# Some filler matmuls moved onto the two 64-row halves of the array, between the score matmuls; a new table of steps; three filler banks in PSUM

## The reference

```
x_proj = silu(xn @ W1 + b1); u, v, q, k = split(x_proj, 4)      # 16 heads of 16
scores = einsum('bqhd,bkhd->bhqk', q, k)
attn   = silu(scores) / S                                        # no softmax
y      = layernorm(einsum('bhqk,bkhd->bqhd', attn, v) * u) @ W2 + b2
h      = gelu(layernorm(xn) @ ternary(w1).T + b1)                # 256 -> 1024
out    = layernorm(h) @ ternary(w2).T + b2                       # 1024 -> 256
x + y + out
```

## Time and profile before

| | |
|---|---|
| median of 3 runs | 1492.84 us |
| the profiled execution | 1493.36 us, span 1491.6 us |
| granted TensorE clock, mean | 0.997 |
| TensorE (PE) busy | 1464.8 us, 98% |
| ScalarE (ACT) busy | 1208.9 us, 81% |
| VectorE (DVE) busy | 895.3 us, 60% |
| chain that ended last | PE 88%, DVE 5%, ACT 4% |

### The profile page before, as it was taken

One profiled execution on the slowest core, in us unless ns is written; L12 is line 12 of the kernel. 1 busy time (PEld: TensorE's weight loads), 2 busy tenths in 40 slices (PEclk: granted clock), 3 DMA queues, 4 the chain that ended last, 5 costly groups with the idle time before them and its releaser, 6 DMA issues.

```text
span 1491.6 us, 25963 instructions
## 1 busy us (share of the span) xinstructions
PE 1464.8 (98%) x9942; PEld 784.7 (53%) x9942; DVE 895.3 (60%) x1719; ACT 1208.9 (81%) x1273; POOL 97.4 (7%) x197
## 2 busy tenths in 40 slices
...
GB/s 248 81 128 57 15 132 65 130 57 15 156 71 100 58 15 156 95 104 29 30 155 99 113 1 59 126 129 84 1 89 110 142 57 5 115 81 142 29 1 29
DMA packets 67996, 123.49 MB, mean 83 GB/s; under 512 B 12832, under 2 KB 14496, under 8 KB 66976
## 3 DMA queue, kind: packets, MB, share of 16 engines
...
q10 hardware_dynamic: 160, 0.26, 0.1%
...
## 4 chain that ended last, share of the span: by engine, by line
PE 88%; DVE 5%; ACT 4%; issue 1%; DVEq 1%; DMA 0%; ACTq 0%
PE outs L1101 30%; PE scores L1079 22%; PE fill L1136 10%; PE fill L1170 9%; PE fill L1154 7%; PE fill L1186 3%; PE fill L1163 3%; ACT attn L636 3%; PE fill L1145 2%; DVE tmp L917 1%; PE fill L1126 1%; DVE hid L900 1%; ACT hid L681 1%; DVE st L813 1%; ACT L636 1%
## 5 line engine op out<-in xcount | busy, mean ns | idle before, releaser
L636 ACT ACTIVATE attn<-scores 128x1024 f32<-128x1024 f32 x1024 | 991.4, 1023 | 225.3 <-PE scores L1079 220.6
L1101 PE MATMUL outs<-attn,V 128*32 128x512 f32 x4096 | 494.3, 600 | 0.0
L1079 PE MATMUL scores<-QS,KS 64*128 64x512 f32 x2048 | 387.7, 452 | 8.3 <-ACT attn L636 7.0
L1079 PEld LDWEIGHTS scores<-QS,KS 64*128 64x128 f32 x2048 | 163.0, 184 | 300.4 <-ACT attn L636 241.5
L1101 PEld LDWEIGHTS outs<-attn,V 128*32 128x32 f32 x4096 | 107.2, 109 | 235.8 <-issue 235.1
L900 DVE SCALAR_TENSOR_TENSOR hid<-fill,ratq,fb1b 128x512 f32<-128x512 f32 x128 | 96.1, 751 | 77.6 <-PE fill L1154 72.3
L917 DVE TENSOR_TENSOR tmp<-fill,l2g 128x512 f32<-128x512 f32 x128 | 88.6, 692 | 88.6 <-PE fill L1163 81.1
L1170 PE MATMUL fill<-Wq,hgh 128*128 128x256 f32 x504 | 128.2, 292 | 2.0 <-DVE hgl L924 1.1
L1136 PE MATMUL fill<-xp,W1h 128*128 128x512 f32 x384 | 128.4, 416 | 0.5 <-DVE xp L949 0.5
L1170 PE MATMUL fill<-Wq,hgl 128*128 128x256 f32 x504 | 123.1, 282 | 0.0
L1170 PEld LDWEIGHTS fill<-Wq,hgh 128*128 128x128 f32 x504 | 95.8, 190 | 18.9 <-issue 14.6
(11 more groups left out here) (138 smaller groups left out, 1349.3 us busy)
## 6 DMA issues: line engine op xcount, KB each, us to landing
...
KS<-k_scratch SPq DMA_DIRECT2D x128, 128.0 KB, 3.2
KS<-k_scratch SPq DMA_DIRECT2D x256, 64.0 KB, 3.4
...
```

The lines of the kernel that those rows point to most:

```text
L636: nc.scalar.activation(attn_of(g)[:, 2 * hf:2 * hf + 2, :], SP[:, 2 * hf:2 * hf + 2, :], ACT.Silu).then_inc(s_silu, 1)
L1079: ins = mm(SP[:, j, :], KS[rows, pair, t * P:(t + 1) * P], QS[rows, pair - c * PPC, h * HALF:(h + 1) * HALF], start=True, stop=True)
L1101: ins = mm(OP[32 * j:32 * j + 32, g // RUN % 2, :], V[:, t, c * HPC // 2 + j, o * DH:o * DH + 2 * DH], attn_of(g)[:, n, :], start=(o == 0 ...
```

## The change

1. **Halves.** Where the pieces of a round are exactly one pair of a kind (`f1.t.0 f1.t.1`, `g.t.0 g.t.1`, `k q`, `u u`) or one `f2` alone, they are issued as matmuls with 64 contraction rows, two side by side, each into a bank of its own (`crossed`, `transposed`, `summed`). The first half of them stands ahead of the first pair of score matmuls of the next group, the second half between the first pair and the second. An `f2` in halves makes two partial sums in two banks, and VectorE adds both. An `f2` in halves waits for both of its `g` at its start; a whole one waited for the second in its middle.
2. **Where the next scores stand.** `scores(2n+2)` is issued at the end of round n instead of the start of round n+1, which is the same place in the stream. On ScalarE the steps of the halved pieces stand between the two SiLU instructions of that group.
3. **Banks.** `outs` has one bank instead of two, so the first `times_v` of each 16 groups waits for VectorE's `output`; `fill` has three banks instead of two. The setup matmuls of block 0 use the third.
4. **Table.** The order is new. In a middle block 11 of the 32 rounds are issued in halves: n = 2 (`k.1.0 q.1.0`), 6 (`u.1.0 u.0.0`), 9 (`k.1.1 q.1.1`), 10 (`f1.0.0 f1.0.1`), 24 and 30 (`k q` of the next block), and 19, 21, 23, 28, 31 (one `f2` each). Round 0 has four `zt` and both of the first `zs`; rounds 1, 3, 4, 5 one `a` each; rounds 7 and 8 one `u` each. Round 25 now has `g.5.0 g.5.1 v.0 gelu.3 v.1 xt.2 ln2.3`, round 26 `xn.3 nrm2.3 v.2 f2.5`; round 15 `f1.5.0 f1.5.1 f2.0 g.1.0 gelu.1 gelu.2 f1.6.0 g.1.1`, round 16 `ln2.1 f1.6.1 f2.1`. In block 0 the first five rounds have no filler piece. The last block has its `g` pairs in halves too.

```diff
-    "vs.1 a.2 zt.3",
+    "k.1.0 q.1.0 zs.2",
...
+def paired(pieces):
+    kinds = [s[0] for x, s in pieces]
+    if kinds == ["f2"]:
+        return SUM_IN_HALVES
+    if len(pieces) != 2 or pieces[0][0] != pieces[1][0]:
+        return False
+    (_, one), (_, two) = pieces
+    return kinds in (["f1", "f1"], ["g", "g"]) and one[1] == two[1] or kinds == ["k", "q"] and one[1:] == two[1:] or kinds == ["u", "u"]
...
-        OP = ctx.enter_context(nc.psum_tensor("outs", [P, 2, HALF], F32))
-        FP = ctx.enter_context(nc.psum_tensor("fill", [P, 2, HALF], F32))
+        OP = ctx.enter_context(nc.psum_tensor("outs", [P, HALF], F32))
+        FP = ctx.enter_context(nc.psum_tensor("fill", [P, FILLS, HALF], F32))
...
# ScalarE, body(b)
+                    nb, ng = next_group(b, 2 * n + 1)
+                    for hf in range(2):
+                        silu_half(b, 2 * n + 1, hf)
+                    steps = list(steps_of(b, n))
+                    group = pieces_of(b, n)[1]
+                    behind = steps.index(group[0]) if group else len(steps)
+                    for x, s in steps[:behind]:
                         step(x, *s)
+                    if nb < NB:
+                        silu_half(nb, ng, 0)
+                    for x, s in steps[behind:]:
+                        step(x, *s)
+                    if nb < NB:
+                        silu_half(nb, ng, 1)
...
# VectorE, step f2
+                    for k, turn in BANKS[x, me]:
+                        dve.drain()
+                        V_.scalar_tensor_tensor(out=part[:, t, :], in0=FP[:, k, 0:D], scalar=cq[:, 1:2],
+                                                in1=part[:, t, :], op0=ALU.mult, op1=ALU.add).then_inc(s_evac[k], 1)
...
# TensorE
-                if g % RUN == 0 and (b or g >= 2 * RUN):
+                if g % RUN == 0 and (b or g):
 
-                    pe.wait_ge(s_z, DC * NH * b + g // RUN - 1)
+                    pe.wait_ge(s_z, DC * NH * b + g // RUN)
...
+            def summed(steps, phase):
+                (x, step), = steps
+                t = step[1]
+                if phase == 0:
+                    wait_free(x, step)
+                pe.wait_ge(s_hg, 2 * T * x + 2 * t + 2)
+                for n in range(4):
+                    for w in (hgh, hgl):
+                        for half, (k, turn) in enumerate(BANKS[x, step]):
+                            rows = slice(half * P // 2, (half + 1) * P // 2)
+                            ins = mm(FP[:, k, 0:D], w[rows, phase, n * P:(n + 1) * P], Wq2[rows, 4 * phase + n, :],
+                                     start=phase == 0 and n == 0 and w is hgh, stop=phase == 1 and n == 3 and w is hgl)
+                            if phase == 1 and n == 3 and w is hgl:
+                                ins.then_inc(s_fill[k], 1)
...
             def body(b):
                 for n in range(ROUNDS):
-                    scores(b, 2 * n)
...
-                    scores(b, 2 * n + 1)
-                    for x, s in steps_of(b, n):
+                    for hf in range(2):
+                        scores(b, 2 * n + 1, hf)
+                    for x, s in full:
                         step(x, *s)
...
+                    for hf in range(2):
+                        if group:
+                            in_halves(group, hf)
+                        if nb < NB:
+                            scores(nb, ng, hf)
```

More of the change, by code:

```diff
@@ L138 @@
 LAST_ROUNDS = {
-    19: "ln2.2 f2.2",
+    19: "f2.2",
     20: "g.3.0 g.3.1 nrm2.2",
@@ L164 @@
 assert sorted(OPENING) == sorted(s for s in ORDER if is_next(s))
-EARLIER = {1: parsed("k.1.0")}
-MOVED = [s for n in sorted(EARLIER) for s in EARLIER[n]]
+SETUP_ROUNDS = 5
+DELAYED = [s for g in range(2 * SETUP_ROUNDS) for s in SLOTS[g] if s[0] in FILLERS and s[0] not in POST and not is_next(s)]
 def steps_of(b, n):
@@ L176, in steps_of @@
         return
-    if b == 0:
-        for s in EARLIER.get(n, ()):
-            yield b, s
+    if b == 0 and n == SETUP_ROUNDS:
+        for s in DELAYED:
+            yield 0, s
     for g in (2 * n, 2 * n + 1):
@@ L431, in last_piece @@
         def last_piece(bank):
-            return [xs for xs in PIECES if bank_of(*xs) == bank][-1]
+            return [xs for xs in PIECES if bank in [k for k, turn in BANKS[xs]]][-1]
         def last_a_tile(i, j):
@@ L730, in _ @@
                         sum_of_abs(i)
+            for hf in range(2):
+                silu_half(0, 0, hf)
+            act.wait_ge(s_const, 3)
+            step(0, "vs", 0)
             for b in range(NB):
@@ new lines, in transposed @@
+            def transposed(steps, phase):
+                if phase == 0:
+                    for x, step in steps:
+                        wait_free(x, step)
+                        wait_data(x, step)
+                for c in range(phase * HC // 2, (phase + 1) * HC // 2):
+                    for half in range(2):
+                        x, (kind, t, r) = steps[half]
+                        k = bank_of(x, (kind, t, r))
+                        toks = slice(half * P // 2, (half + 1) * P // 2)
+                        ins = nc.tensor.transpose(FP[:, k, c * P // 2:(c + 1) * P // 2], hid_of(t)[toks, c * P:(c + 1) * P],
+                                                  ident[toks, toks])
+                        if c == HC - 1:
+                            ins.then_inc(s_fill[k], 1)
@@ L1192, in setup_step @@
                 if g == 0:
+                    wait_evacuated(pe, *[xs for xs in PIECES[:len(OPENING)] if xs in OPENED and bank_of(*xs) == 2][-1])
                     pe.wait_ge(s_abs, 2)
                     pe.wait_ge(s_ones, 1)
-                    mm(OP[:, 1, 0:2], ones[:, :], asum[:, :], start=True, stop=True).then_inc(s_tot, 1)
+                    mm(FP[:, 2, 0:2], ones[:, :], asum[:, :], start=True, stop=True).then_inc(s_tot, 1)
                 elif g == 3:
```

315 lines of the change are left out of this document (197 added, 118 removed).

## The result

The changed kernel takes 1500.28 us (median of 6 runs, 1498.54 to 1504.59); the kernel before, beside it, 1492.94 us. The ratio is 1.0054 (95% interval 1.0042 to 1.0065): it is slower by half a per cent, where the prediction said 1479 and faster.

What follows compares the result with a forecast made beforehand. TensorE matmuls bound full rounds, a TensorE-ScalarE ring of 4.82 us the others. Six middle blocks at -2.3 us give -13.8, both end blocks -0.6: 1493.36 - 14.4 = 1479.0, said as 1479; 80% range 1464 to 1508.

Steps and rivals of the forecast that it cites:

- The floor of 4.82: Rounds with little filler take 4.82 us whatever is in them, as TensorE and ScalarE wait in a ring.
- the emptying stays: Rival: a score load's wait on ScalarE keeps it from loading ahead in halved rounds; +37 us, 1516; chance 0.05.
- the chain of ScalarE through the `gelu` rounds: ScalarE's steps make TensorE wait: rounds 15 and 16 take 16.9 us, rounds 25 and 26 take 16.1.
- ScalarE's price isn't due: Rival: rounds 15, 16, 25, 26 cost as before; -2 us per block more, 1463; chance 0.18.
- a slot of twice 0.118: Rival, dearer halves: 256-column half-height loads run in series; `f2` round 5.0 + 1.7 us, total 1547; chance 0.13.
- 5.28 - 0.42 = 4.86 ... so +0.14, 5.00: Halved `f2` round: saves 0.42 us of shape changes, loses 0.14 waiting for the first SiLU, takes 5.00.
- The `f1` pair likewise 5.0: Round 10, the `f1` pair in halves, takes 5.0 us like a halved `f2` round.
- 6.14 - 0.42 = 5.72: Rounds of `k q` or `u u` in halves fall from 6.14 to 5.72 us.
- So both together -0.6: Blocks 0 and 7: block 0 about -1.3 us; block 7 +1.9 in its last 13 rounds, -1.2 ahead; together -0.6.
- VectorE is late for the `f2` in halves: Rival: `f2` waits for both `g`; four per block, each 0.5 us late, +16 us, 1495; chance 0.14.
- a wait on `hgl`: Sign that would prove the forecast wrong: loads of half-height `f2` matmuls waiting on `hgl`; no size given.
- the way through DRAM that the prediction put at nothing: Next block's `k q` end a round later, with about two and a half rounds' cover before the keys' second half is due.

Runs made afterwards that it cites:

- e9: e11's order in rounds 0 to 22, the order of the kernel before from round 23 on and in the last block: 1474.51 us, ratio 0.9874.
- e5: The changed kernel with the last block's `g` pairs whole and an `f2` in halves waiting for its first `g` only: 1493.82 us, ratio 1.0011.
- e2: The changed kernel with the last block's `g` pairs whole instead of in halves: 1495.7 us, ratio 1.0024.
- e1: The changed kernel, new order and three banks kept, with every piece whole and none in halves: 1510.34 us, ratio 1.0122.
- e7: The changed kernel with every `f2` whole, other pieces in halves, and the last block's `g` pairs whole: 1502.48 us, ratio 1.0077.
- e11: The changed kernel in its new order, with the edits of e2, e3 and e5 together: 1484.25 us, ratio 0.9944.
- e3: The changed kernel with `f1.6.1` back in round 15 and `f2.5` in round 25 (last block: `f2.5` and `ln2.3` back too): 1485.89 us, ratio 0.9951.
- e4: The changed kernel's code with the order table of the kernel before, nothing else changed: 1485.36 us, ratio 0.9951.
- e6: The changed kernel with the order of the kernel before and the edits of e2 and e5: 1482.75 us, ratio 0.993.
- e8: The changed kernel with the order of the kernel before and no halves, leaving only the bank change and its code: 1489.08 us, ratio 0.9974.
- e10: e9 with the second pair's norm `nrm2.1` moved to round 16, ahead of `f2.1`'s sums on VectorE: 1478.69 us, ratio 0.9905.

## Why the prediction was wrong

By its own terms, for the fourth block:

| stretch | predicted | measured |
|---|---|---|
| rounds 0 to 10 | 56.5 | 57.38 |
| 11, 12 | 13.1 | 13.13 |
| 13, 14, 17, 18 | 19.3 | 19.27 |
| 15, 16 | 16.9 | 16.81 |
| 19 to 23 | 24.7 | 25.27 |
| 24 to 31 | 48.4 | 48.80 |

**Right.** The floor of 4.82 held in both kernels. A half-height pair of 256 columns costs 0.119, as one whole matmul; "the emptying stays" fell too. The third bank makes rounds 20 and 22 4.82. Above all the chain of ScalarE through the `gelu` rounds: what was taken out of rounds 15 and 25 came back as a wait in 16 and 26, at 16.81 and 16.00 for 16.9 and 16.1. The rival in which this price wasn't due fell in this order; e9 shows that another order avoids it.

**Slips of the sum.** The rival "ScalarE's price isn't due" starts from 32.3 us for rounds 15, 16, 25 and 26; the rows give 16.21 + 14.12 = 30.33. ScalarE's chain in round 15 adds up to 8.1, not 8.2. "0.4 x 11 x 8" is 35, and a slot of twice 0.118 makes an `f2` round 1.9 longer, not 1.7. None of them moves the forecast by more than 0.1 us a block.

**The failing step, in the middle blocks: the size of a halved round.** "5.28 - 0.42 = 4.86 ... so +0.14, 5.00" was 5.18 to 5.25 for an `f2`; "The `f1` pair likewise 5.0" was 5.47; "6.14 - 0.42 = 5.72" was 5.86. The missing terms of an `f2`: the hand-over behind the first SiLU is 0.08 longer than I had (scores 1.72 behind scores in e5, 1.64 by my sum) and the load behind it 0.08 (701.24 - 700.93 = 0.31 for 0.23 to 0.24). In after itself the wait for both `g` sets the same scores still later, 1.78 behind scores (701.29 - 699.51). The second half of a crossed pair waits for the first, 0.14. And the `f1` pair waits for `y.0`. Three rounds of `k q` or `u u` before round 24 (0.4), the `f1` pair (0.5), three `f2` (0.6) and rounds 24, 28 and 31 (0.5) make 2.0; the rest came out 0.2 shorter, so the block is 1.8 longer than forecast (180.66 for 178.9), 10.6 over six blocks. The waits could be read ahead, in the new code and the new order; I had priced only the one for the SiLU.

**The failing term in the ends: "So both together -0.6"** for blocks 0 and 7, which came out as +8.5 with the start (0.7 + 8.9 - 1.1). Block 7 was summed as +1.9 and -1.2 without its own rows being worked through: the `g` pairs in halves (+0.9 in round 21, +0.9 in 23, about 1.1 in 28; e2 gave 4.6 with the clock), the 1.7 of the clock in round 31, another 1.1 because `f2.6` and `a.1` now share round 28 (28 and 29 take 11.54 in e2, 10.48 before), and rounds 24 to 26, where work was moved out of the `gelu`'s shadow: 21.86 for 18.40, of which 1.5 is the clock. The rival "VectorE is late for the `f2` in halves" named this mechanism and its place on VectorE, but put it, at 0.5 us each, in four rounds of all blocks. By e5 it cost up to 0.09 in most `f2` rounds, 0.33 to 0.38 in one round each of blocks 0, 2, 5 and 6, and 1.0 in rounds of the last block, there for a reason it didn't have, since the `g` were halved themselves. So it was right in a small part, and the sign that the prediction gave for it, a wait on `hgl`, is in the trace.

**Missed altogether: the clock.** No rival had TensorE's clock fall behind the waits that I forecast. Four stretches cost 1.5 to 1.7 each, some 6 us of the 23.3 by which the profiled run is off. The trace of before didn't warn: in the `gelu` rounds of its middle blocks TensorE waits 0.3 us at most, and its clock stays at 1.00. The Trainium skill, "TensorE: Matmul & The Clock Gate", section "HAM oscillation — how this bites in real kernels", describes a kernel whose TensorE falls back to the lower clock in its waits between tiles. There the waits are long ones, for DMA. The rows at 853.98 to 859.59 above agree that waits are followed by it, but here they are under 1 us, for ScalarE, with work between them.

The sum: 10.6 by the fourth block's terms, 3.6 by the other middle blocks and 9.1 at the ends make the 23.3; the clock's 6 us are inside these. Of the 3.6, six rounds make 3.3: round 16 of block 4 (clock, 1.5), its round 1 (0.43; the scores wait 0.38 us for the DMA of `KS`, the way through DRAM that the prediction put at nothing), one late `f2` round each of blocks 2, 5 and 6 (0.28, 0.32, 0.36) and the `f1` pair of block 2 (0.38, behind another stop of VectorE of 0.44).

**Not settled.** Why one block of the same order has a stretch at 1.2 GHz and the next, with the same waits, has not. Apart from those at the start and the end, the traces have 19 stretches at 1.2 GHz. All lie in or behind a `gelu` round (16, 25, 26) or at the end of the last block (after, e1, e2, e5, e7, e11). In 17 of them TensorE stood twice right before, for ScalarE, 0.9 to 1.0 us (2.8 in the last block) and 0.4. e7's longest begins inside the 2.8, and e11's lies behind a single wait of 1.41 us for VectorE, which e3 has too without a stretch. The traces of e3, e4, e6, e8, e9 and e10 have none; in the middle blocks of e4, e6 and e8 single waits of 1.0 to 1.4 us for VectorE are followed by none. That the waits bring the lower clock is argued from this, not shown by a run of its own. Open too is what stops VectorE for 0.43 us.
